# A mean-embedding projection on one core: tiles 1 and 2 start later and in one run, the first mean's work is reordered, and TensorE gets idle products

## What is computed

```python
valid = sequence_ids < 12500                        # ids: 1024 users x 200, drawn from 35..109961
seq_emb = emb_table[where(valid, ids, 0)] * valid   # emb_table: 12500 x 512, float32
user_repr = seq_emb.sum(axis=1) / max(valid.sum(axis=1), 1)
logits = user_repr @ proj_w + proj_b                # proj_w: 512 x 12500 -> out: 1024 x 12500, float32
```

## Time and profile before

| | |
|---|---|
| median of 3 runs | 637.64 us (637.17 to 637.92) |
| the profiled execution's own time | 636.47 us |
| its span in the trace | 634.7 us |
| mean granted TensorE clock | 0.992 |
| TensorE busy | 609.6 us, 96% |
| VectorE busy | 408.0 us, 64% |

### The profile page before, as it was taken

How to read it: one execution, slowest core, us unless ns; L and a number is a source line. 1 busy time by engine, 2 the same in 40 slices (tenths; PEclk the granted TensorE clock), 3 DMA queues, 4 the chain that set the end, 5 groups by cost and what they waited for, 6 DMA issues and landing times.

```text
span 634.7 us, 7598 instructions
## 1 busy us (share of the span) xinstructions
PE 609.6 (96%) x2602; PEld 478.6 (75%) x2602; DVE 408.0 (64%) x723; ACT 145.3 (23%) x161; POOL 230.7 (36%) x227
## 2 busy tenths in 40 slices
PE   1989899999999999999999999999999999999997
PEld 0347568787777777788888888888888888888886
DVE  7988978899879798797885553332333333344442
ACT  8916425141141131300200221111001111111210
POOL 5777878777755667565560000000000000000000
PEclk9988999999999999999999999999999999999999
DMA  9979999999998989798892498445455455556632
GB/s 312 387 255 350 378 395 364 374 318 342 303 326 290 294 293 300 233 324 254 254 334 90 126 291 277 137 141 171 169 177 176 165 178 177 187 186 204 216 125 103
DMA packets 77703, 158.31 MB, mean 249 GB/s; under 512 B 9287, under 2 KB 65042, under 8 KB 77658
## 3 DMA queue, kind: packets, MB, share of 16 engines
q1 hardware_dynamic: 60378, 110.30, 51.1%
q0 software_dynamic: 17280, 47.47, 22.8%
HBM read 115.70 MB, written 51.20 MB: 263 GB/s over the span
## 4 chain that ended last, share of the span: by engine, by line
PE 77%; DVE 14%; issue 4%; DMA 3%; DVEq 0%; ACT 0%; POOL 0%; POOLq 0%
PE acc L845 72%; DVE sums L561 6%; DVE w_lo L625 3%; PE turned L794 3%; DMA rows<-in_L_rec_emb_table_dram,index 3%; DVE key L518 1%; PE turned L786 1%; DVE top L514 1%; PE acc L850 1%; DVE stage L640 1%; DVE sums L558 0%; DMA ids_sb<-in_r_sequence_ids_dram 0%; PE turned L766 0%; DVE count L652 0%; ACT w_hi L422 0%
## 5 line engine op out<-in xcount | busy, mean ns | idle before, releaser
L353 POOL DMA_INDIRECT rows<-in_L_rec_emb_table_dram,index x208 | 220.9, 1062 | 92.0 <-issue 57.6
L640 DVE TENSOR_TENSOR stage<-acc,bias_sb 128x500 f32<-128x500 f32 x162 | 109.3, 676 | 181.3 <-PE acc L845 181.1
L845 PE MATMUL acc<-w_hi,mean_hi 128*128 128x500 f32 x800 | 224.5, 402 | 0.8 <-ACT mean_hi L438 0.8
L845 PE MATMUL acc<-w_hi,mean_lo 128*128 128x500 f32 x800 | 214.5, 390 | 0.4 <-DVE mean_lo L612 0.2
L845 PE MATMUL acc<-w_lo,mean_hi 128*128 128x500 f32 x800 | 214.7, 390 | 0.0
L845 PEld LDWEIGHTS acc<-w_hi,mean_lo 128*128 128x128 f32 x800 | 150.8, 189 | 32.2 <-DVE mean_lo L612 1.2
L845 PEld LDWEIGHTS acc<-w_lo,mean_hi 128*128 128x128 f32 x800 | 150.7, 188 | 31.4
L845 PEld LDWEIGHTS acc<-w_hi,mean_hi 128*128 128x128 f32 x800 | 150.2, 189 | 31.9 <-issue 4.3
L561 DVE SCALAR_TENSOR_TENSOR sums<-rows,mask,sums 128x512 f32<-128x512 f32 x165 | 124.1, 752 | 17.2 <-issue 8.2
L422 ACT ACTIVATE w_hi<-w_raw 128x2000 fp32r<-128x2000 f32 x39 | 72.9, 1874 | 233.5 <-PE acc L845 215.8
L625 DVE TENSOR_TENSOR w_lo<-w_raw,w_hi 128x1000 fp32r<-128x1000 f32 x74 | 85.3, 1194 | 11.7 <-ACT w_hi L422 11.7
(11 more groups left out here) (106 smaller groups left out, 190.1 us busy)
## 6 DMA issues: line engine op xcount, KB each, us to landing
out_dram<-stage SPq DMA_DIRECT2D x200, 250.0 KB, 3.8
w_raw<-in_L_rec_proj_w_dram SPq DMA_DIRECT2D x39, 1000.0 KB, 7.4
bias_sb<-in_L_rec_proj_b_dram SPq DMA_DIRECT2D x39, 250.0 KB, 4.5
raw_at_hi<-in_L_rec_proj_w_dram SPq DMA_DIRECT2D x4, 1000.0 KB, 11.9
rows<-in_L_rec_emb_table_dram,index POOLq DMA_INDIRECT x208, 6.0
raw_at_lo<-in_L_rec_proj_w_dram SPq DMA_DIRECT2D x3, 1000.0 KB, 14.5
stage<-in_L_rec_proj_w_dram SPq DMA_DIRECT2D x1, 1000.0 KB, 26.0
ids_sb<-in_r_sequence_ids_dram SPq DMA_DIRECT2D x1, 700.0 KB, 4.3
```

The source lines that it names most:

```text
L353: return pool.indirect_dma_start(out=dst, out_offset=None, in_=table, in_offset=bass.IndirectOffsetOnAxis(ap=column, axis=0), bounds_check ...
L640: dve.tensor_tensor(stage[:, g % STAGE, r - stores[g][0]], acc[:, r % BANKS, 0:BW], bias_sb[:, i % BIAS], ALU.add).then_inc(s_moved_by_dve, 1)
L845: last = nc.tensor.matmul(bank, first, second, start=part + k == 0, stop=part == 2 and k == K - 1 and not by_act[r])
```

## The change

It has four parts. (1) Tiles 1 and 2 join one and two units later: at their load, the tiles already joined are served first, and then the new tile's five blocks follow in one run. `joined` becomes 0, 11, 24, 35, 51 and on; from unit 29 on the units are the same. VectorE's own columns of tiles 1 and 2 end 1 and 2 units sooner before the join (`behind_others`), that is, at the same unit as before. A fifth bias buffer comes with it. (2) Ahead of the first mean, the left-over rows are summed ahead of column 14 instead of 18, the list for tile 1 is made ahead of column 17 instead of 21, the first step of the mean (now into `mean` itself, the buffer `rest_mean` is gone) stands ahead of `w_low(3)`, and three of tile 2's five sort rounds stand behind `mean_low(0)`. (3) Four idle products stand between tile 0's last column and `turn(0)`, three behind it. (4) Six idle products stand between tile 1's left-over rows and its 8 columns. Idle products write a bank that the next unit to use it starts anew.

```diff
-    RAW, SPLIT, BIAS, ROWS, PLACED, BANKS = 2, 5, 4, 12, 2, 6
+    RAW, SPLIT, BIAS, ROWS, PLACED, BANKS = 2, 5, 5, 12, 2, 6
-    FURTHER_BEHIND, LIST_FIRST_AT, BIAS_DUE = 20, 21, 3
+    SORTED_FIRST = 2
+    OTHERS_FIRST = 2
+    FURTHER_BEHIND, LIST_FIRST_AT, BIAS_DUE = 20, 17, 3
...
-        for t in range(1, TILES):
+        for t in range(OTHERS_FIRST + 1, TILES):
             if JOIN[t] == q:
                 steps += [(x, t, 1) for x in range(start[t], q)]
         here = [t for t in range(TILES) if JOIN[t] <= q < start[t] + NB]
-        steps.append((q, here[0], len(here)))
+        if q in JOIN[1:OTHERS_FIRST + 1]:
+            steps.append((q, here[0], len(here) - 1))
+            steps += [(x, here[-1], 1) for x in range(start[here[-1]], q + 1)]
+        else:
+            steps.append((q, here[0], len(here)))
...
-    LATE_LOAD, REST_FIRST_AT, OPENED = 7, 18, SPLIT - 1
+    LATE_LOAD, REST_FIRST_AT, OPENED = 7, 14, SPLIT - 1
+
+    def behind_others(t):
+
+        return t if t <= OTHERS_FIRST else 0
...
-        begin, end = joined[t - 1] - 2 if t > 1 else 0, joined[t] - SUM_AHEAD
+        begin, end = joined[t - 1] - 2 if t > 1 else 0, joined[t] - behind_others(t) - SUM_AHEAD
...
             sum_further(0)
+            first_further_share()
             w_low(3)
-            for r in range(ROUNDS):
+            for r in range(SORTED_FIRST):
                 sort(2, r)
             first_mean()
             mean_low(0)
+            for r in range(SORTED_FIRST, ROUNDS):
+                sort(2, r)
             for c in range(FAST, FAST + 4):
                 add_column(c)
             fill_slots(1)
...
+            def keep_clock(times, bank, held):
+
+                for _ in range(times):
+                    nc.tensor.matmul(acc[:, bank, 0:BW], held[:, 0:P], held, start=True, stop=True)
...
+            pe.wait_ge(s_w_lo, OPENED)
+            keep_clock(4, SPLIT - 1, w_hi[:, 0, 0])
             turn(0)
+            keep_clock(3, SPLIT - 1, w_hi[:, 0, 0])
...
+                if r == joined[1] - 2:
+                    wait_moved(pe, r - BANKS)
+                    keep_clock(6, r % BANKS, mean_hi[:, 0, 0:BW])
```

More of the change, by code:

```diff
@@ L157, in mean_embedding_projection @@
         rest_rows = sb("rest_rows", [P, HID], F32)
-        rest_mean = sb("rest_mean", [P, HID], F32)
         rows = sb("rows", [P, ROWS, HID], F32)
@@ L448, in rest_share @@
                 act.wait_ge(s_rest, t + 1)
-                nc.scalar.activation(rest_mean[:], turned[:], ACT.Copy,
+                nc.scalar.activation(mean[:], turned[:], ACT.Copy,
                                      scale=inv_count[:, t:t + 1]).then_inc(s_rest_mean, 1)
@@ L592, in sum_further, with first_further_share @@
                 add_further(t)
+            def first_further_share():
+                dve.tensor_scalar(mean[:], sums[:], inv_count[:, 0:1], None, ALU.mult).then_inc(s_further_mean, 1)
             def first_mean():
-                dve.tensor_scalar(rest_mean[:], sums[:], inv_count[:, 0:1], None, ALU.mult).then_inc(s_further_mean, 1)
                 dve.wait_ge(s_further_mean, 1)
@@ L599, in first_mean @@
                 dve.wait_ge(s_added, len(pe_columns[0]))
-                dve.scalar_tensor_tensor(mean[:], turned[:], inv_count[:, 0:1], rest_mean[:], ALU.mult,
+                dve.scalar_tensor_tensor(mean[:], turned[:], inv_count[:, 0:1], mean[:], ALU.mult,
                                          ALU.add).then_inc(s_mean, 1)
@@ L606, in mean_of @@
                 dve.wait_ge(s_rest_mean, t)
-                dve.scalar_tensor_tensor(mean[:], sums[:], inv_count[:, t:t + 1], rest_mean[:], ALU.mult,
+                dve.scalar_tensor_tensor(mean[:], sums[:], inv_count[:, t:t + 1], mean[:], ALU.mult,
                                          ALU.add).then_inc(s_mean, 1)
```

## The result

The changed kernel takes 642.14 us (median of 5 runs, 641.78 to 644.35) against 637.31 us for the kernel before (5 runs, 636.72 to 637.92). The ratio is 1.0085, 95% interval 1.007 to 1.010: it is slower, by more than the 0.5% forecast. The profiled execution is one of the longer ones (642.99 us, span 641.2 us), so its trace shows 6.5 us more than the trace of before, where the medians differ by 4.8. Nearly all of the 6.5 us stands in one wait and what follows it.

What follows compares the result with a forecast made beforehand. TensorE's chain of products (busy 96%), taking turns with VectorE's fixed list, was taken as the bound; 1.7 us lateness plus 1.6 us clock on 637.64 gave 640.9 us, own range 639.2 to 641.9, wider range 635.6 to 642.4.

Steps and rivals of the forecast that it cites:

- The 1.7 us of lateness at tile 3's mean: Tile 3's mean on VectorE: it starts 1.7 us late, at 167.7 instead of 166.04; bounds 1.2 to 2.5 us.
- the 1.6 us of clock: TensorE at tile 3's turn: half clock in or behind the wait adds 1.6 us; bounds 0.4 to 1.65 us.
- the sum of 3.3 us: Whole kernel: 1.7 us of VectorE's lateness plus 1.6 us of clock, making the median 640.9 us.
- The rival in which the wait costs no clock: Tile 3's mean: TensorE's wait costs no clock, leaving 1.7 us of lateness, 639.3 us; chance 0.14.
- The row with 1.00 at the start: First 20 us: granted clock reads 1.00 with TensorE working 5.88; by it a long pause need cost nothing, sum 1.7 us.
- The first mean, 1.4 us sooner: Tile 0's join: last column ends at about 44.9 and `turn(0)` comes at 45.75 instead of 47.15, 1.4 us sooner.
- 0.5 us, by which tile 1's turn was to be late: Tile 1's join: the mean ends at 88.9 + 0.75, so `turn(1)` comes at 89.7 instead of 89.18.
- The wait of 2 us for ScalarE's share: Ahead of tile 2's mean: VectorE idles 2 us for ScalarE's share, the mean starting at 128.4 instead of 126.05.
- the 0.6 us taken off for the move of unit 21: VectorE ahead of tile 2's mean: one more move, unit 21's, cuts its lag from 2.35 to 1.7 us.
- The forecast that TensorE would reach tile 3's turn near 163.4 and wait 5 us: Tile 3's join: TensorE arrives at 163.4 instead of 166.05 and waits 5 us for `turn(3)` at 168.5.
- The diagonals: Tile 1's join: ScalarE makes them behind its move of unit 7, half a us later than before, at some 77.2.
- the forecast's own range: Whole kernel: 639.2 to 641.9 us from the bounds of lateness and clock; the forecast's chance was 0.47.

## Why the prediction came out as it did

The direction, the place and the chain of causes stood: VectorE late from the sort rounds, one unit of lead on TensorE, VectorE idle at tile 2's mean, TensorE idle at tile 3's, the clock down behind it. What failed is the size of both terms of the sum. The 1.7 us of lateness at tile 3's mean was 4.1 us in the profiled execution, beyond its bound of 2.5, and the 1.6 us of clock was 2.4, beyond its bound of 1.65. So the sum of 3.3 us became 6.5 there, and 4.8 by the medians or 5.4 by the ratio, which is also just outside the range. Three steps led to this, all off to the same side, and one row was misread.

- **The clock, 1.6 us, measured 2.4, and 1.3 to 2.6 in other runs.** The step said that a pause is followed by 3.2 to 3.3 us at half clock, as in the earlier trace rows, and its bound was 1.65. Behind the pause of 6.2 us the clock was at half for 6.8 us in all, and 5.3 of them fell on work. The two rows came from pauses of 1 to 2 us; I took their length over to a wait three times as long. The rival in which the wait costs no clock was wrong. The rule of the Trainium skill ("TensorE: Matmul & The Clock Gate", Part 1: The HAM clock gate), that an engine without work falls and is let up only by sustained work, agrees with these rows.
- **The row with 1.00 at the start** was read wrongly. In the same 20 us TensorE's weight loads come 0.8 us and more apart up to 18.80 and 0.43 apart from there on, while the row says 1.00 throughout. Loads of 0.34 us, 0.85 us apart, stand at 34.25 and 35.10 too, where the granted clock reads 0.50. So TensorE ran at half rate there, behind a first wait of 12.4 us, and the row was no evidence that a long pause is free:

```profile
17.13 0.34 PEld L794 LDWEIGHTS turned<-rows,diags_at_hi 128*128 128x128 f32 x1 [0.52 <-issue]
17.98 0.34 PEld L794 LDWEIGHTS turned<-rows,diags_at_hi 128*128 128x128 f32 x1 [0.52 <-issue]
18.80 0.19 PEld L794 LDWEIGHTS turned<-rows,diags_at_hi 128*128 128x128 f32 x1 [0.49 <-issue]
19.23 0.19 PEld L794 LDWEIGHTS turned<-rows,diags_at_hi 128*128 128x128 f32 x1 [0.24 <-issue]
```

- **The first mean, 1.4 us sooner, measured 0.5.** The step moved 0.86 us of work out of the way of the last columns and took them to end at 44.9. They ended at 45.70, because the rows came at their own pace once the backlog was gone. TensorE's own gain there has no worth (the run with the idle products alone shows it), but VectorE's new list starts behind that mean: `w_low(4)` is 1.6 us late instead of 0.65, tile 1's mean 2.1 us instead of 0.65. Moving the rounds alone gives all of it. In the sum this was 0.5 us, by which tile 1's turn was to be late; the turn came at 91.13 instead of 89.18, 1.95 us late. It is the step that counts most: 1.45 of the 2.4 us by which the lateness was mis-sized.
- **Tile 2's mean and the one move that counts for VectorE.** The wait of 2 us for ScalarE's share was measured at 1.80 and 1.38. But the 0.6 us taken off for the move of unit 21 were not seen: from tile 2's mean to tile 3's VectorE takes 39.99 us before, 39.96 with the joins alone and 40.34 in the changed kernel, with one move less in each of the two. Small waits between (0.34 us for tile 3's list among them) are new in their place; I haven't added them up. The joins' lateness of 1.5 us plus the rounds' 2.0 give 3.5 of the 4.1 us seen at tile 3's mean. The other 0.6 us stay open. Part of it is no more than executions differ (the run with idle products at tile 3, whose VectorE queue is the same, has that mean at 169.72, 0.44 us sooner). And with the sort rounds ahead and all the rest of the change kept the mean is 2.4 us late, not 1.5, so the other edits may have a share.

The forecast that TensorE would reach tile 3's turn near 163.4 and wait 5 us was near: it was there at 164.75 and waited 6.22. The diagonals came at 79.3 rather than 77.2 and the columns' end at 87.6 rather than 85.85; moving the sort rounds alone brings them to 78.64 and 86.88, so much of it is that lateness. The idle products by themselves came to nothing (1.0001). The fifth bias buffer was never run without the late joins or the rest of the change, so that it costs nothing is not shown. The upper end of the forecast's own range, 641.9, is a slip: the bounds add up to 641.8.

## What to carry to other kernels

When an order is shifted to keep one engine fed at one join, the lead must have somewhere to go at each later join. Here the first join that stayed where it was took it all back, with a fall of the clock on top, at tile 3 and, when tile 3 had moved too, at tile 4. Before work is moved behind a milestone on the engine that has no slack, ask when the milestone itself can come; if its inputs arrive at their own pace, the milestone stays and the work is simply late. And ask what stands behind a stretch at half clock: ahead of a wait for another engine or a transfer it cost next to nothing here, and ahead of TensorE's own chain it cost 1.3 to 2.6 us.

## What the hardware did that I had not expected

The price of a pause depended on when in it the clock fell, and not on its length alone. Behind pauses of 1 to 2 us the trace of before has the clock at half for 3.4 us at a time (the windows of the earlier trace rows lie a little inside). Four traces have a wait of about 6 us for a mean, and in each of them it was at half for 6.8 us, in one piece. How much of that lay behind the turn, where it costs, differed (us; the last column is the time to the next tile's turn, over that of a kernel without a fall there):

| kernel | wait | fall, into the wait | half clock behind the turn | lost |
|---|---|---|---|---|
| the changed one, tile 3 | 6.22 | 4.7 | 5.3 | 2.4 |
| sort rounds back ahead, tile 3 | 6.22 | 2.3 | 2.9 | 1.3 |
| late joins alone, tile 3 | 5.83 | 4.8 | 5.8 | 2.6 |
| tile 3 late too, tile 4 | 6.39 | 4.1 | 4.5 | 1.9 |

Two waits of the same 6.22 us cost 2.4 and 1.3 us. That would also fit the spread of the changed kernel's own times, 641.78 to 644.35 us, but only one of these executions has a trace. And 26 products whose results nobody reads, put into that pause, kept the clock up; they were worth 1.6 us by the medians in a kernel of 640.
